# Three-layer diffusion transformer on one core: attention ticks reordered and dealt out anew, skew rows loaded ahead of the weights

## The reference, cut to what matters

```python
# L0: U = qr(P); R = expm(skew(silu(cond) @ W.T + b)); x = x + ((x U) R - x U) U^T
# each of three layers (16 heads of 18 channels; layer 1 of the kernel also normalises q and k):
h = layernorm(x) * (1 + scale) + shift
q, k, v = split(h @ w_qkv + b_qkv)
attn = softmax(q @ k.T * hd ** -0.5)
x = x + gate * ((attn @ v) @ w_proj + b_proj)
h = layernorm(x) * (1 + scale2) + shift2
x = x + gate2 * (gelu(h @ w1 + b1) @ w2 + b2)   # layer 2 of the kernel: top 2 of 4 experts
```

## Time and profile before

| | us |
|---|---|
| median of three runs | 2028.12 |
| the profiled execution | 2027.6 |
| its span in the trace | 2025.8 |
| opening until the first attention exponential | 281.1 |
| attention of layers 0, 1, 2 | 269.7, 302.9, 268.9 |
| MLP of layers 0, 1, 2 | 195.9, 179.0, 528.3 |

### The profile page before, as it was taken

The page is one execution under the profiler, slowest core; times in us unless marked ns, Lnnn a source line. Parts: engine busy times, 40 slices in busy tenths (PEclk is TensorE's granted clock), DMA queues, the critical chain, the costliest instruction groups (busy, mean ns, idle before and its releaser), DMA issues.

```text
span 2025.8 us, 28803 instructions
## 1 busy us (share of the span) xinstructions
PE 1828.4 (90%) x10144; PEld 1233.4 (61%) x10144; DVE 1203.5 (59%) x2585; ACT 958.8 (47%) x1744; POOL 587.5 (29%) x597
## 2 busy tenths in 40 slices
PE   7799589999899789999889999999989899999998
PEld 6676344444387664444338765444347788898897
DVE  5675267777355568777625467777724555555554
ACT  2332247665745348776654416775753432222221
POOL 3453222232365433332334412322322211101000
PEclk9999679999799899999879989999979999999999
DMA  7000133333100122322310203323201010001000
GB/s 245 13 1 2 38 118 90 102 90 91 45 11 1 50 84 77 105 73 76 96 30 7 65 18 117 105 84 95 85 2 45 18 33 18 30 12 36 1 24 24
DMA packets 69598, 114.29 MB, mean 56 GB/s; under 512 B 15091, under 2 KB 30115, under 8 KB 69167
## 3 DMA queue, kind: packets, MB, share of 16 engines
q1 hardware_dynamic: 69456, 112.45, 18.1%
HBM read 81.19 MB, written 30.73 MB: 55 GB/s over the span
## 4 chain that ended last, share of the span: by engine, by line
PE 70%; ACT 10%; DVE 7%; issue 4%; DMA 4%; SPq 3%; POOL 1%; ACTq 0%; DVEq 0%; POOLq 0%
PE ps L1663 23%; PE ps L1747 13%; PE ps L1716 8%; PE ps L1702 7%; PE ps L1812 5%; PE ps L1684 4%; ACT Pr L1498 3%; PE ps L1787 2%; ACT xn L1392 2%; PE ps L1547 1%; DVE negmax L1069 1%; ACT HQ L1473 1%; PE ps L1536 1%; DMA heads_t<-stage 1%; DMA raw<-in_w 1%
## 5 line engine op out<-in xcount | busy, mean ns | idle before, releaser
L1069 DVE TENSOR_REDUCE negmax<-ps 128x1 f32<-128x512 f32 x768 | 490.5, 684 | 184.1 <-PE ps L1684 178.4
L1498 ACT ACTIVATE Pr<-ps 128x512 f32<-128x512 f32 x768 | 406.8, 601 | 149.0 <-PE ps L1702 147.7
L1509 ACT ACTIVATE g<-ps,b1col 128x512 f32<-128x512 f32 x216 | 148.5, 687 | 450.2 <-PE ps L1663 437.4
L1258 DVE CAST G<-g 128x512 fp32r<-128x512 f32 x216 | 127.1, 588 | 324.2 <-ACT g L1509 323.3
L1702 PE MATMUL ps<-QK 55*128 55x512 f32 x768 | 248.9, 514 | 54.5 <-ACT Pr L1498 52.2
L1747 PE MATMUL ps<-W2a,G 128*128 128x288 f32 x1728 | 267.2, 305 | 2.0 <-DVE G L1260 2.0
L1747 PEld LDWEIGHTS ps<-W2a,G 128*128 128x128 f32 x1728 | 249.1, 194 | 14.5 <-DVE G L1260 4.2
L1702 PEld LDWEIGHTS ps<-QK 55*128 55x128 f32 x768 | 97.8, 194 | 244.2 <-ACT Pr L1498 147.2
L1684 PE MATMUL ps<-QK 54*128 54x512 f32 x768 | 199.6, 434 | 33.9 <-DVE negmax L1069 14.8
L1716 PE MATMUL ps<-Pr,V 128*32 128x512 f32 x1536 | 220.9, 649 | 0.0
L1260 DVE TENSOR_TENSOR G<-g,G 128x512 fp32r<-128x512 f32 x216 | 167.0, 773 | 7.4
(11 more groups left out here) (212 smaller groups left out, 2522.5 us busy)
## 6 DMA issues: line engine op xcount, KB each, us to landing
QK<-heads_t SPq DMA_DIRECT2D x192, 144.0 KB
heads_t<-stage SPq DMA_DIRECT2D x96, 252.0 KB
QK<-heads_t SPq DMA_DIRECT2D x192, 72.0 KB
raw<-in_w SPq DMA_DIRECT2D x18, 432.0 KB
raw<-in_w SPq DMA_DIRECT2D x12, 576.0 KB
WA<-in_ada_w SPq DMA_DIRECT2D x3, 1728.0 KB
heads_t<-stage SPq DMA_DIRECT2D x24, 144.0 KB
QK<-W1a SPq DMA_DIRECT2D x192, 2.0 KB, 2.5
```

The source lines that it names most:

```text
L1069: dve.tensor_reduce(negmax[:, m % 2, t, h:h + 1], ps[:, row_bank(l, s, i), :], AX, ALU.max, negate=True).then_inc(a_free, 1)
L1258: dve.tensor_copy(G[:, n % 3, 0, :], g32[:, n % 2, :]).then_inc(g_hi, 1)
L1498: act.activation(Pr[:, t % 2, 2 * half + pair, :], ps[:, (16 * s + u) % 3, :], ACT.Exp, scale=SCALE).then_inc(b_free, 1)
L1509: act.activation(g32[:, n % 2, :], ps[:, 4, :], ACT.Gelu if l == 1 else ACT.Gelu_apprx_tanh, bias=b1col[:, e, s % FT:s % FT + 1]).then_inc ...
```

## The change

- On TensorE, ScalarE and VectorE the tick's scores, exponentials and maxima now stand ahead of the other items of the tick; on VectorE `out` stays in front.
- In attention, proj tiles (and qk tiles outside layer 1) are formed in two ticks: the first takes matmuls 0 to 3 of qk or the first half of proj, the second the rest; the other engines read the tile in the second.
- `scale_rows` is split over four ticks in attention.
- The ticks of qk, v, proj, ln, tok, turn and max are dealt out anew. `turn` goes from tick 3 to tick 7 of a step, but for the first step of a block.
- SyncE issues the skew rows right behind X; pieces 0 and 1, WA, WP and qkcol come after them.

```diff
     for g in range(4):
         s = 4 * b + g
         if s + 1 < STEPS:
-            out.append((8 * g + 1, "max", l, s + 1, 0))
+            out.append((8 * g, "max", l, s + 1, 0))
         if s > 0:
-            out += [(8 * g + 1, "out", l, s - 1, 0), (8 * g + 3, "turn", l, s - 1, 0)]
-    proj = (6, 8, 10, 16) if l != 1 else (7, 13, 16, 19)
+            out += [(8 * g + 1, "out", l, s - 1, 0), (8 * g + (3 if g == 0 else 7), "turn", l, s - 1, 0)]
     if z >= 0:
-        out += [(proj[t], "proj", l, z, t) for t in range(TT)]
+        out += [(t, "proj", l, z, k) for k, t in enumerate((6, 10, 14, 18) if l != 1 else (10, 12, 18, 20))]
     if y < B:
-        out += [(t, "place", l, y, g) for g, t in enumerate((8, 16, 26 if l == 1 else 24, 32))]
         if l != 1:
-            out += [(t, "qk", l, y, j) for j, t in enumerate((2, 4, 12, 19, 26))]
-            out += [(t, "v", l, y, k) for k, t in enumerate((14, 21, 22, 24))]
+            out += [(t, "place", l, y, g) for g, t in enumerate((8, 16, 24, 32))]
+            out += [(t, "qk", l, y, j) for j, t in enumerate((2, 4, 12, 20, 22))]
+            out += [(t, "v", l, y, k) for k, t in enumerate((1, 9, 17, 25))]
         else:
-            for k, t in enumerate((0, 2, 3, 5)):
+            out += [(t, "place", l, y, g) for g, t in enumerate((11, 16, 24, 32))]
+            for k, t in enumerate((1, 2, 3, 5)):
...
-            out += [(t, "qk", l, y, j) for j, t in enumerate((4, 6, 12, 23, 28))]
-            out += [(t, "v", l, y, k) for k, t in enumerate((10, 11, 14, 15))]
+            out += [(t, "qk", l, y, j) for j, t in enumerate((7, 9, 14, 17, 27))]
+            out += [(t, "v", l, y, k) for k, t in enumerate((4, 6, 15, 22))]
...
-        out += [(12 if l == 1 else 20, "mean1", l, y2, 0)]
-        out += [(t, "ln1", l, y2, c) for c, t in enumerate((18, 20, 21) if l == 1 else (27, 28, 30))]
+        out += [(12 if l == 1 else 18, "mean1", l, y2, 0)]
+        out += [(t, "ln1", l, y2, c) for c, t in enumerate((23, 25, 26) if l == 1 else (26, 27, 29))]
...
-        out += [(t, "ln2", l, 0, c) for c, t in enumerate((19, 21, 23))]
+        out += [(t, "ln2", l, 0, c) for c, t in enumerate((21, 23, 25))]
...
+def in_parts(t, kind, l):
+    return TICKS[t][0] == "a" and (kind == "proj" or kind == "qk" and l != 1)
...
+        at, parts = t + LAG[engine][key[0]], in_parts(t, key[0], key[1])
+        if engine == "PE":
+            out[at].append((*key, (0, 1) if not parts else (0,)))
+            if parts:
+                out[at + 1].append((*key, (1,)))
+        else:
+            out[min(at + parts, len(TICKS) - 1)].append(tuple(key))
...
-            for l in range(LAYERS):
-                sp.dma_start(WA[l][:, 0:2, :], a["ada_w"][l, 0:256, :].rearrange("(s p) n -> p s n", p=128)).then_inc(ada_in[l], 16)
-                sp.dma_start(WA[l][0:34, 2, :], a["ada_w"][l, 256:C + 2, :]).then_inc(ada_in[l], 16)
...
-            load_piece(0)
-            load_piece(1)
-            sp.dma_start(WP[:, :, :], a["w_proj"][0]).then_inc(wp_in, 16)
-            sp.dma_start(qkcol[:, :, :], a["qkcol"]).then_inc(col_in, 16)
             sp.wait_ge(skew_ev, 1)
...
+            load_piece(0)
+            load_piece(1)
+            for l in range(LAYERS):
+                sp.dma_start(WA[l][:, 0:2, :], a["ada_w"][l, 0:256, :].rearrange("(s p) n -> p s n", p=128)).then_inc(ada_in[l], 16)
+                sp.dma_start(WA[l][0:34, 2, :], a["ada_w"][l, 256:C + 2, :]).then_inc(ada_in[l], 16)
+            sp.dma_start(WP[:, :, :], a["w_proj"][0]).then_inc(wp_in, 16)
+            sp.dma_start(qkcol[:, :, :], a["qkcol"]).then_inc(col_in, 16)
             load_piece(2)
...
-                for key in todo[tick]:
+                first = [key for key in todo[tick] if what != "a" or key[0] == "out"]
+                for key in first:
                     work(*key)
                 if what == "a" and s + 2 < STEPS:
                     negmax_unit(l, s + 2, 2 * u)
                     negmax_unit(l, s + 2, 2 * u + 1)
+                for key in todo[tick]:
+                    if key not in first:
+                        work(*key)
...
             for tick, (what, l, s, u) in enumerate(TICKS):
-                for key in todo[tick]:
-                    work(*key)
                 if what == "a":
                     exp_unit(l, s, 2 * u)
                     exp_unit(l, s, 2 * u + 1)
-                elif what == "m" and u == 0 and s < EXPERTS[l] * B * FT:
+                for key in todo[tick]:
+                    work(*key)
+                if what == "m" and u == 0 and s < EXPERTS[l] * B * FT:
                     gelu_tile(l, s)
...
-            def seven(o, lhs, rhs, rows):
-                for p in range(7):
+            def seven(o, lhs, rhs, rows, parts=(0, 1)):
+
+                for p in range(0 if 0 in parts else 4, 7 if 1 in parts else 4):
...
-                    for g in range(4):
+                    for g in range(0 if 0 in parts else 2, 4 if 1 in parts else 2):
...
-                for key in todo[tick]:
-                    work(*key)
-                if what == "m" and u == 1 and s >= 2:
-                    back(l, s - 2)
                 if what == "a":
                     for i in (2 * u, 2 * u + 1):
                         key_scores(l, s, i)
...
+                for key in todo[tick]:
+                    work(*key)
+                if what == "m" and u == 1 and s >= 2:
+                    back(l, s - 2)
```

More of the change, by code:

```diff
@@ L103, in attention_window @@
     if y2 < B:
         out += [(4 + t, "stats1", l, y2, t) for t in range(TT)]
-        out += [(12 if l == 1 else 20, "mean1", l, y2, 0)]
-        out += [(t, "ln1", l, y2, c) for c, t in enumerate((18, 20, 21) if l == 1 else (27, 28, 30))]
+        out += [(12 if l == 1 else 18, "mean1", l, y2, 0)]
+        out += [(t, "ln1", l, y2, c) for c, t in enumerate((23, 25, 26) if l == 1 else (26, 27, 29))]
         if l == 1:
-            for k, t in enumerate((24, 26, 27, 29)):
+            for k, t in enumerate((28, 29, 30, 31)):
@@ L109, in attention_window @@
                 out += [(t, "tok", l, y2, k), (t + 2, "var", l, y2, k)]
-            out += [(31, "root", l, y2, 0), (33, "inverse", l, y2, 0)]
+            out += [(33, "root", l, y2, 0), (35, "inverse", l, y2, 0)]
     if b == 0:
@@ L236, in items @@
             out += [(MT[l] + 2 * FT * v + t, *key) for t, *key in rows]
-    out += [(t + 3, "scale", l, b, 1 + (kind == "mean2")) for t, kind, l, b, k in out if kind in ("mean1", "mean2")]
+    for t, kind, l, b, k in [x for x in out if x[1] in ("mean1", "mean2")]:
+        out += [(t + 3 + (i if TICKS[t][0] == "a" else 0), "scale", l, b, TT * (kind == "mean2") + i) for i in range(TT)]
     return sorted(out, key=lambda x: x[0])
@@ L289, in agenda @@
     for t, *key in ITEMS:
-        if key[0] in LAG[engine]:
-            out[min(t + LAG[engine][key[0]], len(TICKS) - 1)].append(tuple(key))
+        if key[0] not in LAG[engine]:
+            continue
+        at, parts = t + LAG[engine][key[0]], in_parts(t, key[0], key[1])
[5 more added lines that the diff above has]
+            out[min(at + parts, len(TICKS) - 1)].append(tuple(key))
     return out
@@ L1382, in hold, with scale_rows @@
                 return act32[:, h % 2, :]
-            def scale_rows(key):
+            def scale_rows(key, t):
                 i, (kind, l, b, k) = NORM[key], key
-                act.wait_ge(rstd_ready, i + 1)
-                if i > 0:
-                    what, pl, pb, pk = NORM_KEYS[i - 1]
-                    act.wait_ge(misc_full, MISC["ln" + what[-1], pl, pb, 2] + 1)
-                for t in range(TT):
-                    act.activation(xn[:, t, 0:C], X[:, TT * b + t, :], ACT.Identity, bias=shift[:, t:t + 1],
-                                   scale=rstd[:, t:t + 1]).then_inc(xn_part, 1)
+                if t == 0:
+                    act.wait_ge(rstd_ready, i + 1)
+                    if i > 0:
+                        what, pl, pb, pk = NORM_KEYS[i - 1]
+                        act.wait_ge(misc_full, MISC["ln" + what[-1], pl, pb, 2] + 1)
+                act.activation(xn[:, t, 0:C], X[:, TT * b + t, :], ACT.Identity, bias=shift[:, t:t + 1],
+                               scale=rstd[:, t:t + 1]).then_inc(xn_part, 1)
+                if t < TT - 1:
+                    return
                 act.wait_ge(xn_part, TT * (i + 1))
@@ L1434, in work @@
                 if kind == "scale":
-                    scale_rows(("mean1" if k == 1 else "mean2", l, i, 0))
+                    scale_rows(("mean1" if k < TT else "mean2", l, i, 0), k % TT)
                     return
@@ L1752, in back, with work @@
                     ins.then_inc(g_used, 1)
-            def work(kind, l, i, k):
+            def work(kind, l, i, k, parts):
                 key = (kind, l, i, k)
@@ L1779, in work @@
                 n = MISC[key]
-                if n > 0:
+                if n > 0 and 0 in parts:
                     pe.wait_ge(misc_free, n)
```

(5 more changed lines are left out.)

## The result

The changed kernel takes 2018.12 us (median of 20 runs, 2000.62 to 2027.76) against 2027.92 us of the kernel before (20 runs, 2019.52 to 2035.36): ratio **0.9941, interval 0.9923 to 0.9958**, 12 us or 0.6% faster. Forecast were 42 us. The profiled execution has a span of 2016.5 us, 9.3 less than before. Single executions differ by 1.3%, so the places of the time are read block by block and the verdicts from ratios.

The account below looks back on a forecast made before the run. TensorE was taken as close to full in attention, uneven ticks leaving it waiting 6.1 of 69.6 us in layer 0's block 1. 2027.6 - 34.0 (attention) - 7.6 (opening) = 1986.0 us; range 1960 to 2012, by block bounds 1962 to 2003.

Parts of the forecast that it names:

- waits only move: Rival, chance 0.09: in attention each gap is passed on, only the opening gains; 2020 us.
- The opening: Before attention: skew rows issued right behind X end VectorE's 7.67 us wait before its mask; -7.6 us.
- The swap of order is mostly a relabelling: Attention: scores ahead of a tick's items leave TensorE's and ScalarE's sequences the same if items move one tick earlier; 0.
- Halves, the price: Attention: nine more tiles a block entered and left between score tiles, 0 to 0.07 us a change; at most 0.6 a block.
- the drain rival: Rival, chance 0.05: split qk and proj tiles add 132 changes that drain the array, 0.16 us each, 21 us; 2007 us.
- Halves, the gains: Layers 0 and 2, blocks 0, 1, 2: split tiles even out ticks and cut TensorE's waiting; -3.5, -3, -2 us.
- Layer 1: Layer 1's attention blocks 0 to 2: new deal takes part of about 12 us idle each, a clump staying; -3, -4, -3 us.
- Later turn: Layer 1's attention: VectorE's 8.6 us wait for proj before `turn` goes; 1 us credited in each of three blocks.
- Scale in four ticks: Attention: each of four activations adds about 0.55 us to a tick, covered by split tiles' ticks; counted within other gains.
- Block 3: Last attention block: first w1 piece's split stands a tick later, shortening its DMA wait; -2, -3, -2 us for three layers.
- The MLPs at nothing: MLP ticks, 903.9 us: each engine keeps its sequence, so no change in time.
- The signs said ahead: Trace signs: mask near 52 us, layer 0 blocks 61, 66.5, 64 us, shorter key waits; wrong if half qk over 1.2.

Follow-up runs that it names:

- skew_only: The kernel before with only SyncE's new DMA order (skew rows right behind X, pieces 0 and 1, WP, qkcol after): 2018.77 us, ratio 0.9956.
- layer1_before: The changed kernel with layer 1 dealt as before (ticks one earlier), its proj whole, its ln1 scale in one tick, turn still late: 1998.91 us, ratio 0.9865.
- spill_after_max: The changed kernel with SyncE's spill of the last qk tile one tick later outside layer 1, behind the maximum row's placing: 2018.82 us, ratio 0.9967.
- scale_lump: The changed kernel with the four activations of `scale_rows` in one tick again: 2020.63 us, ratio 0.9986.
- early_spill_layer1: The changed kernel with the edits of layer1_before and spill_after_max, and an MLP's first two weight pieces loaded four ticks earlier: 1987.24 us, ratio 0.9791.
- spill_layer1: The changed kernel with the edits of layer1_before and spill_after_max together: 2010.22 us, ratio 0.9917.

## Why the prediction was wrong in size

The sign was right, and the opening. The 1986.0 us lay 32 us too low, and the measured time outside the range. The time is that of "waits only move" (2020 us, to which 0.09 was given), but not by its mechanism: TensorE's waits did shrink, and other costs took their place. In the profiled execution the 32.3 us are made up so (forecast, measured): blocks 0 to 2 of layers 0 and 2 -17.0, +2.5; those of layer 1 -10.0, +9.7; blocks 3 -7.0, -23.0; the opening -7.6, -4.3; the MLPs 0, +5.9. What the blocks 3 gave beyond the 7 us goes in large part with the clock, and was luck: without it the miss would have been larger.

- **The opening, -7.6.** Right in mechanism and size: -8.0 us at the end of the reductions, skew_only 0.9956, 9 us. In the profiled execution 3.7 of the 8.0 us are gone again by the first exponential, beside the lower clock; in the other kernels with this opening 5.7 to 8.4 us were left there.
- **"The swap of order is mostly a relabelling", 0.** Not tested by itself. layer1_before, whose layer 1 has the old ticks one earlier, fits it: 73.4, 77.9 and 68.3 us against 75.2, 78.5 and 69.4.
- **Halves, the price of 0 to 0.07 us a change of tile.** This term was mis-sized: 0.17 to 0.20 us a split tile, 1.6 us a block where "0.6 a block" stood, 12 us in all. More than half of the miss is in the count: nine tiles more "are entered and left", which is 18 changes, as the drain rival counted them, and 18 x 0.07 is 1.3 us, but the sum took nine. The rest is the size, about 0.10 us a change. The row that I trusted, the pair behind a qk tile at 0.33 us, shows only the time after the start of the next tile; the cost lies at the first and the last step of a tile, and the tile of seven matmuls in the MLP (1.63 us against 1.83) showed it. The rival had the mechanism with 21 us. Beside this stands the Trainium skill, TensorEngine Tiling (Array Packing), Key Properties: a change of tiling mode, not just of tile, drains the engine. The trace agrees in direction: about 0.10 us for each change between score tiles and full tiles, none between full tiles of different kinds. Whether the 54 or 55 rows or the mode as such costs it was not separated.
- **Halves, the gains of 3.5, 3 and 2 us.** The waiting fell nearly as forecast in block 1 (2.4 of 6.1 us, 3 forecast), but net block 1 gave 0.8, block 0 1.4 (layer 2, clock 1.00), and block 2 *lost* 3 us. Over the three blocks of a layer the keys' wait for exponentials, 6.4 us, fell by 5.5 us, where 8.5 us of gain was forecast; against them stand about 4.4 us for 23 split tiles (an estimate, 23 x 0.19) and the new wait of 3.7 us in layer 0, 3.5 in layer 2. The step that failed in block 2: I costed TensorE, ScalarE and VectorE by tick and left SyncE out. Moving the last qk from tick 26 to 22 moved its spill ahead of the maxima on a queue that goes in order. spill_after_max shows it: 69.2 to 65.6.
- **Layer 1, -3, -4, -3.** Measured +5.0, +0.1, +4.6. The prediction saw the clump at ticks 7 to 9 and still took a gain. Only the idle time of 12 us or so stood behind the 10 us, and the range by the block bounds, 1962 to 2003, let only layers 0 and 2 vary: with nothing gained in layer 1 either it would have reached 2013. Undoing the deal gave 15 us. Which of its pieces costs most stays open: the placing at tick 11 shows waits of 0.95 and 0.94 us in blocks 0 and 2, and the lower clock stands beside them.
- **Later turn, 1 us x 3.** The wait of 8.6 us went, as forecast. layer1_before keeps the late turn; with the relabelled deal its three blocks are 3.4 us below those of before. That fits the 3, but the gain wasn't tested alone, and there VectorE's wait for proj in reading it rose from 16.7 to 25.3 us: the wait had moved.
- **Scale in four ticks.** 9 us in the ratio, by scale_lump, of which 0.6 to 0.7 us a block can be read at full clock.
- **Block 3, -2, -3, -2, "between +3 and -13".** Measured -8.4, -12.9 and -1.7 in one execution, much of it clock: 0.81, 0.77 and 0.81 before, 0.98, 0.95 and 0.82 after. The step itself held in the changed kernel: the waits for the piece fell from 3.2, 7.4 and 2.7 us to 0, 5.1 and 0. But it held in layers 0 and 2 beside the maxima's wait, which let block 3 begin late. The load is dated by a DMA that waits for landings, and not by block 2's end: in spill_after_max the 3.6 us won in block 2 came back as 5.45 us of ScalarE's wait. So this term and that of block 2 could not both be had, which the sum took for granted. early_spill_layer1 against spill_layer1 shows it, 26 us.
- **The MLPs at nothing.** The sequence kept its ticks. Of the +2.5 and +4.2 us in two of them no cause was found; layer 2's MLP ran at a clock of 0.98 both times, and takes 526 to 533 us over the kernels tried, which all have the same.
- **The signs said ahead.** Mask at 52 us, turn's wait gone, the keys' wait for exponentials shorter (6.4 to 0.9 us in layers 0 and 2, 9.8 to 5.5 in layer 1) with ln's still 1.9, a half qk tile under 1.2 us (1.12) and keys behind a half at 0.33: all right, and none of them told of the 12 us. A sign has to be the sum from start to start of both halves. One sign of being wrong did come, more half clock, before attention (0.56 against 0.71) and in layer 1's block 0 (0.83 against 0.95). The blocks of layer 0 were to be 61, 66.5 and 64 and are 64.0, 68.8 and 69.2.

That the final version stands at 1987.24 us, beside the 1986.0 forecast, is no proof of the forecast's steps: its sum has other terms.

## What to carry to other kernels

When items are dealt out anew by hand, write down the new order of *every* queue, the DMA issuer's above all: one item moved by four ticks put its spill ahead of a small urgent transfer, and that cost 3.6 us a block. Price a split tile by the start-to-start sum of its parts, count the way in and the way out, and look for the same tile in other company elsewhere in the trace. Expect a gain in one stage to be met by the next stage's transfer: issue that transfer ahead of anything that waits, before judging the first gain, since the three edits that moved the changed kernel's 0.9941 to 0.9865, 0.9967 and 0.9909 alone moved it to 0.9791 together.
